# Softmax weights of a causal attention, split into halves by turns: two units of three by ScalarE and GpSimd, the third and the end by VectorE

## The reference

```python
def _L0_attn_ref(x, Wq, Wk, Wv, Wo, bo):       # 16 heads of 64, S = 2048
    q, k, v = (x @ Wq), (x @ Wk), (x @ Wv)     # split into heads
    logits = einsum('nhid,nhjd->nhij', q, k) / 8 + causal
    attn = softmax(logits)
    out = einsum('nhij,nhjd->nhid', attn, v)
    return out @ Wo + bo
...
x = layernorm(x + _L0_attn_ref(x, ...))
x = layernorm(x + _L0_ffn_ref(x, ...))         # ternary weights, 128 -> 512 -> 128
x = layernorm(x + _L1_attn_ref(x, ...))        # quantised attention
x = layernorm(x + _L1_ffn_ref(x, ...))         # 16 experts, top 1, capacity 128
```

## Time and profile before

| | |
|---|---|
| median of 3 runs | 1072.24 us (1070.28 to 1078.67) |
| profiled execution | 1072.05 us, span 1070.3 us |
| TensorE busy | 831.1 us, 78% of the span |
| VectorE busy | 765.5 us, 72% |
| ScalarE busy | 694.1 us, 65% |
| GpSimd busy | 550.7 us, 51% |
| mean granted TensorE clock | 0.903 of full speed |

### The profile page before, as it was taken

How to read it: one execution, slowest core, us unless ns; L and a number is a source line. 1 busy time by engine, 2 the same in 40 slices (tenths; PEclk the granted TensorE clock), 3 DMA queues, 4 the chain that set the end, 5 groups by cost and what they waited for, 6 DMA issues and landing times. The chain is left out here.

```text
span 1070.3 us, 26775 instructions
## 1 busy us (share of the span) xinstructions
PE 831.1 (78%) x10709; PEld 550.4 (51%) x10709; DVE 765.5 (72%) x1317; ACT 694.1 (65%) x952; POOL 550.7 (51%) x420
## 2 busy tenths in 40 slices
PE   4577888889888988897898989888999677544290
PEld 2234555556555555564565556556566566324290
DVE  6577888788778868896887788688955746756114
ACT  3245677678677767776786777678799576434163
POOL 1024556456456556564665556556688565321540
PEclk8679999899899999998999999899999988655596
DMA  5400220031003101200210031013000510003252
GB/s 153 94 10 16 56 52 2 16 73 34 15 13 72 26 17 41 66 2 16 65 42 7 12 76 32 16 31 69 9 3 2 176 35 2 1 1 84 64 182 82
DMA packets 58419, 47.19 MB, mean 44 GB/s; under 512 B 9514, under 2 KB 54696, under 8 KB 58166
## 3 DMA queue, kind: packets, MB, share of 16 engines
q1 hardware_dynamic: 57270, 44.01, 16.5%
q0 software_dynamic: 1024, 1.45, 0.4%
HBM read 15.59 MB, written 5.26 MB: 19 GB/s over the span
## 5 line engine op out<-in xcount | busy, mean ns | idle before, releaser
L535 POOL TENSOR_TENSOR prob_lo<-prob,prob_hi 128x736 f16<-128x736 f32 (+3 forms) x320 | 455.7, 1429 | 373.5 <-ACT prob L433 372.0
L429 ACT ACTIVATE prob_hi<-psum 128x1024 f16<-128x1024 f32 (+1 forms) x320 | 293.5, 917 | 199.5 <-PE psum L357 197.1
L465 DVE TENSOR_REDUCE part_max<-psum 128x2 f32<-128x1024 f32 (+1 forms) x320 | 329.4, 1052 | 73.8 <-PE psum L323 43.5
L433 ACT ACTIVATE prob<-psum 128x1024 f32<-128x1024 f32 (+1 forms) x320 | 293.4, 918 | 0.0
L354 PE MATMUL psum<-q_hl,k_hh 128*128 128x512 f16 (+3 forms) x640 | 230.5, 360 | 69.3 <-DVE part_max L465 22.8
L500 DVE TENSOR_TENSOR prob_lo<-prob,prob_hi 128x288 f16<-128x288 f32 (+3 forms) x320 | 240.5, 753 | 56.7 <-ACT prob L433 55.9
L371 PE MATMUL psum<-v,prob_hi 128*128 128x65 f16 x2176 | 234.2, 194 | 4.5 <-POOL prob_lo L535 3.2
L375 PE MATMUL psum<-v,prob_lo 128*128 128x65 f16 x2176 | 234.1, 196 | 0.0
L373 PE MATMUL psum<-v,prob_hi 128*128 128x64 f16 x2176 | 233.1, 193 | 0.0
L357 PE MATMUL psum<-q_hm,k_l 65*128 65x512 f16 (+3 forms) x640 | 225.2, 357 | 0.0
L371 PEld LDWEIGHTS psum<-v,prob_hi 128*128 128x128 f16 x2176 | 204.0, 99 | 33.4 <-issue 12.3
(11 more groups left out here) (221 smaller groups left out, 1028.7 us busy)
## 6 DMA issues: line engine op xcount, KB each, us to landing
k_hh<-kq_hi SPq DMA_DIRECT2D x128, 64.0 KB
ew<-in_L_ffn_W SPq DMA_DIRECT2D x32, 256.0 KB
q_hl<-kq_hi SPq DMA_DIRECT2D x64, 64.0 KB
q_hl<-kq_lo SPq DMA_DIRECT2D x64, 64.0 KB
k_l<-kq_lo SPq DMA_DIRECT2D x64, 64.0 KB
q_hm<-kq_hi SPq DMA_DIRECT2D x64, 64.0 KB
expert_rows<-heads_out SPq DMA_DIRECT2D x1, 1032.0 KB, 8.3
e_xe<-expert_rows SPq DMA_DIRECT2D x4, 258.0 KB, 3.7
```

The source lines that it names most:

```text
L429: act.activation(m.prob_hi[i % HI_RING][:, 0:u.width], src, ACT.Exp, scale=EXP_SCALE)
L433: act.activation(m.prob[i % PROB_RING][:, 0:u.width], src, ACT.Exp, scale=EXP_SCALE)\
L465: last = dve.tensor_reduce(m.part_max[:, g % 2, :, r, c:c + 1], src[:, :, col:col + width], AX, ALU.max)
L535: pool.tensor_tensor(m.prob_lo[i % LOW_RING][:, c], m.prob[i % PROB_RING][:, c], m.prob_hi[i % HI_RING][:, c], ALU.subtract).then_inc(low_ ...
```

## The change

The columns of a unit are no longer shared. A unit with index i, i mod 3 = 0 or 1 and i < 286 goes to GpSimd (`on_pool`): ScalarE takes both exponentials as before, and GpSimd subtracts over the whole width; VectorE has no part in it. Every other unit, i mod 3 = 2 and the last 34, goes to VectorE: ScalarE takes only the 32-bit exponential, VectorE casts it to f16 into `prob_hi` (`high`) and subtracts over the whole width (`low`). The cast stands where the subtraction stood, ahead of the jobs of the step; the subtraction comes behind the step's maxima. `weigh` and ScalarE's reuse of a `prob` buffer wait for the one engine that has the unit.

```diff
-    def share(u):
-        return u.width // 64 * (32 if u.index >= NU - LEAD else 18)
+    def on_pool(u):
+        return u.index < NU - LEAD and u.index % 3 != 2
+
+    def lows(index):
+        mine = [on_pool(u) for u in UNITS[:index + 1]]
+        return sum(mine), len(mine) - sum(mine)
+
+    def wait_low(engine, index):
+        by_pool, by_dve = lows(index)
+        if on_pool(UNITS[index]):
+            engine.wait_ge(low_pool, by_pool)
+        else:
+            engine.wait_ge(low_dve, by_dve)
...
             def weigh(u):
-                pe.wait_ge(low_dve, u.index + 1)
-                pe.wait_ge(low_pool, u.index + 1)
+                wait_low(pe, u.index)
...
-                act.activation(m.prob_hi[i % HI_RING][:, 0:u.width], src, ACT.Exp, scale=EXP_SCALE)
+                if on_pool(u):
+                    act.activation(m.prob_hi[i % HI_RING][:, 0:u.width], src, ACT.Exp, scale=EXP_SCALE)
                 if i >= PROB_RING:
-                    act.wait_ge(low_dve, i - PROB_RING + 1)
-                    act.wait_ge(low_pool, i - PROB_RING + 1)
+                    wait_low(act, i - PROB_RING)
                 act.activation(m.prob[i % PROB_RING][:, 0:u.width], src, ACT.Exp, scale=EXP_SCALE)\
                     .then_inc(free[u.buf], 1)
...
+            def high(u):
+                i, c = u.index, slice(0, u.width)
+                dve.wait_ge(free[u.buf], u.turns + 1)
+                if i >= HI_RING:
+                    dve.wait_ge(weighed, i - HI_RING + 1)
+                dve.tensor_copy(m.prob_hi[i % HI_RING][:, c], m.prob[i % PROB_RING][:, c]).then_inc(high_dve, 1)
+
             def low(u):
-                i = u.index
-                dve.wait_ge(free[u.buf], u.turns + 1)
+                i, c = u.index, slice(0, u.width)
+                dve.wait_ge(high_dve, lows(i)[1])
                 if i >= LOW_RING:
                     dve.wait_ge(weighed, i - LOW_RING + 1)
-                c = slice(0, share(u))
...
             for i in range(NU):
-                low(UNITS[i])
+                if not on_pool(UNITS[i]):
+                    high(UNITS[i])
                 if i > 1 and UNITS[i - 2].last:
                     invert(UNITS[i - 2])
                 if i > 0:
                     run(PLAN[i - 1], ("kq", "v"))
                 run(PLAN[i], ("max", "shift"))
+                if not on_pool(UNITS[i]):
+                    low(UNITS[i])
                 if i > 1 and UNITS[i - 2].last:
                     normalise(UNITS[i - 2])
...
             for u in UNITS:
+                if not on_pool(u):
+                    continue
...
-                c = slice(share(u), u.width)
+                c = slice(0, u.width)
```

More of the change, by code:

```diff
@@ L259, in attention @@
     high_done = sem("high_done")
+    high_dve = sem("high_dve")
     spread = [[sem(f"spread{i}{c}") for c in range(4)] for i in range(3)]
```

## The result

The changed kernel takes 1114.84 us (median of 4 runs, 1113.02 to 1115.57) against 1072.28: a ratio of 1.0384, 95% interval 1.0339 to 1.0429. The change costs 42.6 us. The forecast was 1084; its direction and its range held, its size was less than a third of what came.

A forecast was written before the change was run, and what follows sets the result against it. No engine was full in the middle; afterwards a loop of GpSimd, VectorE, weighing and exponentials was to bind there, VectorE at the end. Middle + 5 and end + 6 on 1072 gave 1083, rounded up to 1084 us; range 1066 to 1100.

The forecast's parts named there:

- The added wait: TensorE's weighing waits for VectorE's whole subtraction, some 50 to 90 us in total where it was 3.2.
- the third rival: VectorE's cast runs at one column a cycle like the subtraction, giving 1099 or 1100 us; chance 0.10.
- The key chain: Key/query chain that TensorE waits for: 41 us of waits, 0.15 us a unit, of which 0.14 stay.
- The end: Last 34 units: VectorE becomes the bound with cast and whole subtraction, 1.73 us a unit; + 6 us.
- the loop: Middle: GpSimd's subtraction, VectorE's subtraction, weighing, next step's scores, exponentials, GpSimd again; mean 6.70 us for three units, 2.23 each.
- The sum 2.23 + 0.08 + 0.05 + 0.14: Middle, us a unit: loop mean, further jobs, ScalarE's key and value casts, key chain waits; 2.50 against 2.48.
- the old waits: TensorE's middle waits: VectorE's maxima 23 us, to fall by about half; ScalarE's exponentials 14, a third to go; key chain 41.
- the term + 5 us: Middle, 268 units at 0.02 us more each, 2.50 against 2.48: + 5 us.
- The second rival: Middle: the loop's wait adds to the old waits, + 0.14 us a unit or 38 us; 1116 us; chance 0.20.
- the case above 1%: Total time above 1083 us, from half of the forecast's chance, the added waits and the slow cast; chance 0.45.
- The first rival: VectorE is first at the port shared with GpSimd, so the loop doesn't close; 1041 us; chance 0.25.

The follow-up runs named there:

- Experiment 6: Changed kernel, with GpSimd made to wait, for every third unit, until VectorE's whole subtraction of the unit before is done; 1078.43 us.
- experiment 2: Changed kernel, with GpSimd subtracting only the first 64 columns of each of its units, the rest of the low half left at zero; 1052.51 us.

## Why the prediction was right in kind and wrong in size

**Right.** The chain of waits that the prediction described is there: GpSimd is first by some tenths of a microsecond, VectorE's subtraction waits for it to end, weighing waits for VectorE. Experiment 6 shows it by order alone, experiment 2 by length alone. It is there in 51 of 95 units, though, where the sum had it in all. The added wait was to be 50 to 90 us in total; by the matmul rows, from which the prediction took its 3.2, it is 46.0, a little less, and by the weight loads 58.3 in the middle and 73.8 with the end. The new durations held: whole GpSimd subtraction 2.13 us (446.50 in the changed kernel: 2.13), whole VectorE subtraction 1.22 (1225 ns), cast 0.69 (684 ns), so the third rival, the slow cast, is out. The key chain kept its waits (35.5 and 35.1 us), the maxima's fell by less than half, the exponentials' by a fifth. The end was put at + 6 and measured + 3.5. A full unit there was put at 1.95 to 2.0 us with its share of the scaling; in the trace it takes 1.86 without a scaling and 2.19 with one (casts at 828.06 and 830.25), once in five units, so 1.93 in the mean: the scaling costs 0.33 us where it was put at 0.6.

**Wrong: the step from the loop to the pace of the middle.** The sum 2.23 + 0.08 + 0.05 + 0.14 = 2.50 us a unit took the loop's mean as the new pace and set it against 2.48, a term of + 5 us. It held the old waits to be swallowed: "What VectorE is relieved of comes back as one long wait per triple." The account of the weight loads says otherwise: 58.3 us came on top and only 19.3 went. Measured are 2.61 us a unit; the term + 5 us came out as + 39 (+ 36 from unit 12 on). The pace is above the loop's mean although the loop closes in only 51 of 95 units, so the loop doesn't set the pace: each time it closes it adds to the old one. Why the old waits weren't swallowed is my reading and no run parts it: the steps of this kernel differ (second jobs, key and value jobs), and a step that is late in the loop doesn't win the time back in one that waits for something else.

The second rival made that sum, old pace plus added wait minus what goes, and gave 38 for the 39. That it met the number so well is luck: it added 0.29 us a unit, 78 us, where 58.3 were added, and took off 16 us of old waits and 24 of overlap, where 19.3 went and no overlap shows. Its form is right, its terms are not. I gave it 0.20 for no better reason than that overlap seemed likelier, with no row that showed any overlap. The chances were also added up wrongly: half of the forecast's 0.45 with 0.20 and 0.10 is 0.52 for the case above 1%, not 0.45.

**Smaller faults.** The waits were read from TensorE's matmul rows (23 for maxima, 14 for exponentials), which show the smaller part; the weight loads' rows show 50.6 and 26.7 to 765 us. And ScalarE's wait for a `prob` buffer, 45.7 us in the middle, was missing from the list of those who wait for VectorE's subtraction, though the wait stands in `exponents`. How much of the 39 us passes through it isn't settled: a fourth `prob` buffer would part it from the weighing's wait, and no run has one. ScalarE's busy time was to fall by 115 to 118 us and fell by 96.1 (694.1 to 598.0): the exponentials are listed with 1.02 us but follow each other at 0.92, so each that goes frees less than its length. It doesn't bear on the time.

**The first rival** (VectorE first, 1041) was not what happened, but experiment 6 made it so, and gave 1078.4. That the next cast then waits was right (1008 ns), and its time was too low by 37 us: the key chain, the maxima (39.3 us by the weight loads) and part of the subtraction's wait (32.6) stayed.

**What the change was bound to miss.** Before, the two engines excluded each other for a short time on every unit; the change makes that rarer and each instance longer: GpSimd 2.13 us at a time for 1.58, VectorE 1.22 us for some 0.46 (an estimate from the 0.69 us of 512 columns and the 1.22 of 1024). ScalarE, which was relieved, had caused 26.7 us of TensorE's stops in the middle, and 4.9 of them went. Halves of the old split do the opposite, shorter exclusive stretches with more work in all, and won 24 us.

## What to carry to other kernels

Where two engines share an exclusive resource, the length of one instruction on it is a cost of its own: splitting the less urgent engine's instruction in two won 24 us here, where this redistribution of the work lost 43. A split too many can lose again: quarters cost 6 us against halves on the kernel before, in the stretch where GpSimd is the later of the two, though on the changed kernel they still won 5. A new wait is to be added to the old pace in full unless a row shows which old wait it will lie over; the length of a loop is not a pace when only some steps close it. And TensorE's waits are to be read from the weight loads, whose idle time added up to the loss here, and not from the matmuls behind them alone.

## What the runs showed of the hardware

A VectorE instruction that waits for GpSimd's end is let in between two GpSimd instructions that stand one behind the other: with halves in the changed kernel VectorE's subtraction ended at 142.34 us, between GpSimd's halves that ended at 141.25 and 143.35, and the longest stop of TensorE for it fell from 2.4 to 1.4 us. The cast within SBUF (f32 to f16, 1024 columns) takes 0.68 us alone and is kept out by GpSimd as well: with VectorE's subtraction put first, its mean rose from 690 to 1008 ns; in the Trainium skill, SBUF — State Buffer, section "SBUF: two separate sides", the exclusive lock holds against a VectorE copy in a two-port mode too, and these runs agree. An extra GpSimd subtraction costs little of itself: 640 instructions for 320 cost 69 us of its listed time, 0.22 us each. Its forms of 276 and 736 columns, 0.70 and 1.58 us, give 0.17 us as the fixed part, an estimate.
